# Router products cut into pieces between the query matmuls, with the first norm application and the first scatters moved, in an attention and mixture-of-experts kernel

## What is computed

```python
def attn(x, context, ...):                       # 16 heads of 32
    q = x @ Wq.T + bq; k = context @ Wk.T + bk; v = context @ Wv.T + bv
    scores = einsum('bhtd,bhcd->bhtc', q, k) / sqrt(32)
    return einsum('bhtc,bhcd->bhtd', softmax(scores), v) @ Wo.T + bo

def ffn(x, ...):                                 # 8 experts, the best 2 of each token
    router_weights = softmax(x @ W_router.T + b_router)
    topk_w, topk_idx = top_k(router_weights, 2)
    ...
    expert_out = einsum('bsd,eod->bseo', x, W_experts) + b_experts
    return einsum('bseo,bse->bso', expert_out, router_weights)

x = x + attn(layernorm(x), ctx, ...)
x = x + ffn(layernorm(x), ...)
```

## Time and profile before

| what | value |
| --- | --- |
| timed runs | median 1279.43 us of 3 (1275.38 to 1282.6) |
| profiled execution: span from first to last instruction | 1340.9 us |
| mean granted clock of TensorE | 0.950 |
| busy, PE / DVE / ACT / POOL | 1224.7 / 881.3 / 722.1 / 744.6 us |
| DMA | 239.22 MB, mean 178 GB/s |

### The profile page before, as it was taken

The page is one execution under the profiler, slowest core; times in us unless marked ns, Lnnn a source line. Parts: engine busy times, 40 slices in busy tenths (PEclk is TensorE's granted clock), DMA queues, the critical chain, the costliest instruction groups (busy, mean ns, idle before and its releaser), DMA issues. The chain is left out here.

```text
span 1340.9 us, 36001 instructions
## 1 busy us (share of the span) xinstructions
PE 1224.7 (91%) x11024; PEld 735.1 (55%) x11025; DVE 881.3 (66%) x1933; ACT 722.1 (54%) x1040; POOL 744.6 (56%) x980
## 2 busy tenths in 40 slices
PE   8887999998999989999999986869899999999997
PEld 4445665655655655665655654534354555555454
DVE  4657787877868867867877867545445555555454
ACT  4336875775775775775766662624333333334333
POOL 4003555675675675675675674864644445444545
PEclk9879999999989998989989997889999999999999
DMA  8842664584583574583583573967999989998886
GB/s 267 253 135 65 173 176 153 148 254 142 150 258 130 142 241 152 147 262 131 144 237 115 132 215 109 357 221 156 199 177 184 175 173 188 179 172 155 168 165 133
DMA packets 135547, 239.22 MB, mean 178 GB/s; under 512 B 18440, under 2 KB 49416, under 8 KB 134280
## 3 DMA queue, kind: packets, MB, share of 16 engines
q1 hardware_dynamic: 102391, 161.24, 41.2%
q0 software_dynamic: 29808, 67.73, 25.2%
q10 hardware_dynamic: 3232, 8.68, 1.9%
HBM read 112.00 MB, written 101.40 MB: 159 GB/s over the span
## 5 line engine op out<-in xcount | busy, mean ns | idle before, releaser
L1854 PE MATMUL S<-we_s,wq_s 128*128 x1620 | 376.3, 382 | 12.6 <-DVE att L1832 5.8
L1782 POOL DMA_INDIRECT out<-xn,to x135 | 208.9, 1547 | 212.7 <-DMA out<-xn,to 123.6
L1854 PEld LDWEIGHTS S<-we_s,wq_s 128*128 128x128 f16 x1620 | 158.1, 98 | 180.8 <-issue 22.3
L1172 POOL TENSOR_TENSOR we_s<-P_s,we_s 128x1024 f16<-128x1024 f32 x96 | 204.2, 2136 | 65.6 <-ACT we_s L927 65.3
L1793 ACT ACTIVATE wq_s<-PVp 128x512 f16<-128x512 f32 x137 | 81.6, 597 | 272.4 <-PE PVp L1844 247.1
L1252 POOL DMA_INDIRECT dispatched<-xn,idx x128 | 131.7, 1029 | 92.6 <-ACT xn L620 52.1
L975 DVE TENSOR_REDUCE mx_sb<-S 128x6 f32<-128x924 f32 x160 | 171.3, 1111 | 11.3 <-PE S L726 9.1
L708 PE MATMUL W<-we_s,wq_s 128*128 128x512 f16 x512 | 168.7, 409 | 8.7 <-ACT mT L933 5.3
L746 PE MATMUL W<-wo_s,aT_hi 128*128 128x512 f16 x512 | 164.5, 383 | 2.6 <-DVE aT_lo L953 1.4
L1832 DVE SCALAR_TENSOR_TENSOR att<-S,be_s 128x512 f32<-128x512 f32 x135 | 93.3, 691 | 111.0 <-PE S L1854 101.5
L1810 DVE TENSOR_TENSOR wq_s<-PVp,wq_s 128x512 f16<-128x512 f32 x137 | 94.6, 691 | 38.3 <-ACT wq_s L1793 35.1
(11 more groups left out here) (207 smaller groups left out, 2039.8 us busy)
## 6 DMA issues: line engine op xcount, KB each, us to landing
P_s<-dispatched SPq DMA_DIRECT2D x139, 260.5 KB
we_s<-we_s SPq DMA_DIRECT2D x186, 128.0 KB, 6.0
be_s<-in_x SPq DMA_DIRECT2D x16, 1024.0 KB, 9.1
xR_s<-in_x SPq DMA_DIRECT2D x16, 1024.0 KB
out<-xR_s SPq DMA_DIRECT2D x16, 1024.0 KB
wst<-in_weT SPq DMA_DIRECT2D x16, 512.0 KB, 6.2
we_scratch<-wsp SPq DMA_DIRECT2D x16, 512.0 KB, 5.5
Kst<-k_scratch SPq DMA_DIRECT2D x16, 480.0 KB, 5.1
```

The lines of the kernel that those rows point to most:

```text
L1172: e.tensor_tensor(Pst[1][:, r:r + 2, :], exps(n), Pst[0][:, r:r + 2, :], ALU.subtract).then_inc(pldp, 1)
L1782: e.indirect_dma_start(out, bass.IndirectOffsetOnAxis(ap=to[u][:, :], axis=0), yw[u % YW], None, bounds_check=N - 1, oob_is_err=False, com ...
L1854: m = e.matmul(Yp[:, u % 2, :], gT[u % 2][xp][:, k, :], we_s[:, bass.ds(n * WN + (wp * KC + k) * D, D)], start=(c == 0), stop=(c == 11))
```

## The change

- LA and LB become steps for one token tile each (`pe_LA(e, b, j)`, `pe_LB(e, b, j)`), called by a new `pe_logits`. Pieces 0 and 1 stand behind MT, piece 2 behind Q6 and piece 3 behind Q7. LA leaves its place between ST4 and AT2, and is done for block `bp2`, at the end of the slot before.
- LA moves from bank 1 to bank 0, beside LB (columns 64 to 127). Q9 of the next slot waits for RA, AT2 no longer does; the semaphore for LB is now that of the first reduction (`lbs`).
- DVE: RA runs right after the first reduction of RB, and the rest of RB is a step RL of its own behind it.
- ACT: NY0 and NY1 come before Qh of the first query group, NY2 and NY3 behind it, ahead of NX0; before, all four stood behind the second group and the expert weights' high part.
- POOL: BX3 moves ahead of the first norm's chain NC, so that SC stands right behind the low parts PL7 and PL8.

```diff
@@ -63,7 +63,7 @@
 R32 = 3
 
 BANK = {
-    "ST0": 2, "ST1": 3, "ST2": 2, "Q9": 0, "AT0": 1, "ST3": 3, "AT1": 0, "ST4": 2, "LA": 1, "AT2": 1, "AT3": 0,
+    "ST0": 2, "ST1": 3, "ST2": 2, "Q9": 0, "AT0": 1, "ST3": 3, "AT1": 0, "ST4": 2, "LA": 0, "AT2": 1, "AT3": 0,
     "ST5": 3, "XT0": 0, "O0": 1, "ST6": 2, "R": 0, "ST7": 3, "XT1": 1, "XT2": 0, "ST8": 2, "ST9": 3, "XT3": 1,
     "O3": 0, "Q0": 1, "MX0": 2, "MX1": 3, "Q3": 0, "MX2": 2, "MX3": 3, "O6": 1, "MX4": 2, "MX5": 3, "MX6": 2,
     "MX7": 3, "MX8": 2, "O9": 0, "MX9": 3, "MX10": 2, "MT": 1, "LB": 0, "Q6": 1,
@@ -637,9 +637,9 @@
     HOLDERS = {
         0: (
             ("Q9", 1), ("AT1", -1), ("AT3", -1), ("XT0", 2), ("R", -2), ("XT2", 2), ("O3", -1), ("Q3", 2),
-            ("O9", -1), ("LB", -1),),
+            ("O9", -1), ("LB", -1), ("LA", 2),),
         1: (
-            ("AT0", -1), ("LA", 1), ("AT2", -1), ("O0", -1), ("XT1", 2), ("XT3", 2), ("Q0", 2), ("O6", -1),
+            ("AT0", -1), ("AT2", -1), ("O0", -1), ("XT1", 2), ("XT3", 2), ("Q0", 2), ("O6", -1),
             ("MT", 1), ("Q6", 2),),
         2: (
             ("ST0", 0), ("ST2", 0), ("ST4", 0), ("ST6", 0), ("ST8", 0), ("MX0", 1), ("MX2", 1), ("MX4", 1),
@@ -650,7 +650,7 @@
     }
 
     EMPTIED = {"XT": (t1e, 4), "AT": (ate, 4), "Q": (qle, 4), "O": (x1s, 4), "MT": (mte, 1), "R": (rev, 2),
-               "LA": (lae, 1), "LB": (lbe, 4), "MX": (mxr, 11), "ST": (exd, 10)}
+               "LA": (lae, 1), "LB": (lbs, 1), "MX": (mxr, 11), "ST": (exd, 10)}
 
     def emptied(step, s):
 
@@ -823,36 +823,46 @@
         e.wait_ge(nmd, b.at(4, G + 1))
         pe_T(e, f"AT{G}", b, s, lambda j, k: att[:, j, 4 * k:4 * k + 4, :].rearrange("p h d -> p (h d)"), G, atp)
 
-    def pe_LA(e, b, s):
+    LACOL = NJ * 2 * NE
+
+    def pe_LA(e, b, j):
         bank = BANK["LA"]
-        e.wait_ge(t1e, b.at(4, 4))
-        if b.first:
-            e.wait_ge(p_bk, 5)
-        if free := emptied("LA", s):
-            e.wait_ge(*free)
-        for j in range(NJ):
-            o = W[:, bank, j * 2 * NE:(j + 1) * 2 * NE]
-            for k in range(KC):
-                e.matmul(o.rearrange("p (l e) -> p l e", l=2), xnT[0][:, k, j * P:(j + 1) * P], wr_s[:, :, k, :], start=(k == 0), stop=False)
-            for k in range(KC):
-                m = e.matmul(o[:, 0:NE], xnT[1][:, k, j * P:(j + 1) * P], wr_s[:, 0, k, :], start=False, stop=(k == KC - 1))
-        m.then_inc(lap, 1)
-
-    def pe_LB(e, b, s):
+        if j == 0:
+            e.wait_ge(t1e, b.at(4, 4))
+            if b.first:
+                e.wait_ge(p_bk, 5)
+        o = W[:, bank, LACOL + j * 2 * NE:LACOL + (j + 1) * 2 * NE]
+        for k in range(KC):
+            e.matmul(o.rearrange("p (l e) -> p l e", l=2), xnT[0][:, k, j * P:(j + 1) * P], wr_s[:, :, k, :], start=(k == 0), stop=False)
+        for k in range(KC):
+            m = e.matmul(o[:, 0:NE], xnT[1][:, k, j * P:(j + 1) * P], wr_s[:, 0, k, :], start=False, stop=(k == KC - 1))
+        if j == NJ - 1:
+            m.then_inc(lap, 1)
+
+    def pe_LB(e, b, j):
         bank = BANK["LB"]
-        e.wait_ge(ate, b.at(4, 4))
-        if b.first:
-            e.wait_ge(p_rx, 5)
-        if free := emptied("LB", s):
-            e.wait_ge(*free)
-        for j in range(NJ):
-            o = W[:, bank, j * 2 * NE:(j + 1) * 2 * NE]
-            for k in range(KC):
-                e.matmul(o.rearrange("p (l e) -> p l e", l=2), aT[0][:, k, j * P:(j + 1) * P], wx_s[:, :, k, :], start=(k == 0), stop=False)
-            e.matmul(o[:, 0:NE], ones[:, :], cb_r[:, :], start=False, stop=False)
-            for k in range(KC):
-                m = e.matmul(o[:, 0:NE], aT[1][:, k, j * P:(j + 1) * P], wx_s[:, 0, k, :], start=False, stop=(k == KC - 1))
-        m.then_inc(lbp, 1)
+        if j == 0:
+            e.wait_ge(ate, b.at(4, 4))
+            if b.first:
+                e.wait_ge(p_rx, 5)
+        o = W[:, bank, j * 2 * NE:(j + 1) * 2 * NE]
+        for k in range(KC):
+            e.matmul(o.rearrange("p (l e) -> p l e", l=2), aT[0][:, k, j * P:(j + 1) * P], wx_s[:, :, k, :], start=(k == 0), stop=False)
+        e.matmul(o[:, 0:NE], ones[:, :], cb_r[:, :], start=False, stop=False)
+        for k in range(KC):
+            m = e.matmul(o[:, 0:NE], aT[1][:, k, j * P:(j + 1) * P], wx_s[:, 0, k, :], start=False, stop=(k == KC - 1))
+        if j == NJ - 1:
+            m.then_inc(lbp, 1)
+
+    def pe_logits(e, lb, la, j, s):
+
+        if j == 0:
+            if free := emptied("LB" if lb else "LA", s):
+                e.wait_ge(*free)
+        if la:
+            pe_LA(e, la, j)
+        if lb:
+            pe_LB(e, lb, j)
 
     def act_XTh(e, b, i):
         e.wait_ge(t1p, b.at(4, i + 1))
@@ -996,7 +1006,7 @@
         e.wait_ge(nco[0], b.at(NCO, NCO))
         if b.past(2):
             e.wait_ge(rcq, b.at(1, -1))
-        e.tensor_tensor(lga[p][:, :, :], W[:, BANK["LA"], 0:NJ * 2 * NE].rearrange("p (j e) -> p j e", e=2 * NE),
+        e.tensor_tensor(lga[p][:, :, :], W[:, BANK["LA"], LACOL:LACOL + NJ * 2 * NE].rearrange("p (j e) -> p j e", e=2 * NE),
                         st1[p][:, :].rearrange("p (j o) -> p j o", o=1).broadcast_to([P, NJ, 2 * NE]), ALU.mult).then_inc(lae, 1)
 
     def dve_RB(e, b):
@@ -1004,6 +1014,8 @@
             e.wait_ge(g_set, 9)
         e.wait_ge(lbp, b.at(1, 1))
         e.tensor_reduce(lgs[:, :, :], W[:, BANK["LB"], 0:NJ * 2 * NE].rearrange("p (j l e) -> p j e l", l=2, e=NE), AX, ALU.add).then_inc(lbs, 1)
+
+    def dve_RL(e, b):
         e.wait_ge(lbs, b.at(1, 1))
         e.wait_ge(rqd, b.at(2, 2))
         if b.past(1):
@@ -1374,8 +1386,6 @@
             pe_AT(e, bm1, 1, s)
         if on_b:
             pe_ST(e, b, 4, s)
-        if on_bp1:
-            pe_LA(e, bp1, s)
         if on_bm1:
             pe_AT(e, bm1, 2, s)
             pe_AT(e, bm1, 3, s)
@@ -1461,11 +1471,19 @@
             pe_PV(e, b, 5)
         if on_bp1:
             pe_MT(e, bp1, s)
-        if on_bm1 and not bm1.last:
-            pe_LB(e, bm1, s)
+        lb = bm1 if on_bm1 and not bm1.last else None
+        la = bp2 if on_bp2 else None
+        if lb or la:
+            pe_logits(e, lb, la, 0, s)
+            pe_logits(e, lb, la, 1, s)
         if on_bp2:
             pe_Q(e, bp2, 6, s)
+        if lb or la:
+            pe_logits(e, lb, la, 2, s)
+        if on_bp2:
             pe_Q(e, bp2, 7, s)
+        if lb or la:
+            pe_logits(e, lb, la, 3, s)
 
     def act_slot(e, s):
         bm2, bm1, b, bp1, bp2, bp3 = s + (-2), s + (-1), s, s + 1, s + 2, s + 3
@@ -1517,18 +1535,19 @@
             act_PH(e, b, 9)
         if on_bp3 and not bp3.first:
             act_norm(e, 0, bp3)
+        if on_bm2 and not bm2.last:
+            act_NY(e, bm2, 0)
+            act_NY(e, bm2, 1)
         if on_bp2:
             act_Qh(e, bp2, 0)
+        if on_bm2 and not bm2.last:
+            act_NY(e, bm2, 2)
+            act_NY(e, bm2, 3)
         if on_bp3:
             act_NX(e, bp3, 0)
         if on_bp2:
             act_Qh(e, bp2, 1)
             act_WEh(e, bp2)
-        if on_bm2 and not bm2.last:
-            act_NY(e, bm2, 0)
-            act_NY(e, bm2, 1)
-            act_NY(e, bm2, 2)
-            act_NY(e, bm2, 3)
         if on_bp3:
             act_NX(e, bp3, 1)
         if on_bp1:
@@ -1558,6 +1577,10 @@
             dve_SA(e, bp2, 2)
         if on_bm3 and not bm3.last:
             dve_RB(e, bm3)
+        if on_b:
+            dve_RA(e, b)
+        if on_bm3 and not bm3.last:
+            dve_RL(e, bm3)
         if on_bp2 and bp2.past(2):
             dve_SA(e, bp2, 3)
         if on_b:
@@ -1571,8 +1594,6 @@
             dve_ATl(e, bm2, 0)
             dve_NM(e, bm2, 3)
             dve_ATl(e, bm2, 1)
-        if on_b:
-            dve_RA(e, b)
         if on_bm3 and not bm3.last:
             dve_RM(e, bm3)
         if on_bm2:
@@ -1654,13 +1675,13 @@
             pool_RW(e, bm1)
         if on_bp1:
             pool_PL(e, bp1, 5)
+        if on_b:
+            pool_BX(e, b, 3)
         if on_bp4:
             pool_NC(e, bp4, 0)
         if on_bp1:
             pool_PL(e, bp1, 7)
             pool_PL(e, bp1, 8)
-        if on_b:
-            pool_BX(e, b, 3)
         if on_bm1 and bm1.here(NB - 3):
             pool_SC(e, bm1)
         if on_b and not b.last:
@@ -1991,6 +2012,7 @@
             for u in range(4):
                 dve_tile(e, 0, u)
             dve_RB(e, LAST)
+            dve_RL(e, LAST)
             dve_RM(e, LAST)
             for u in range(4, TU):
                 dve_tile(e, 0, u)
@@ -2028,7 +2050,8 @@
             if ND:
                 e.wait_ge(pldd, ND * NB)
             pe_tile(e, 0, 0)
-            pe_LB(e, LAST, LAST + (-(-1)))
+            for j in range(NJ):
+                pe_logits(e, LAST, None, j, LAST + (-(-1)))
             for u in range(1, TU):
                 pe_tile(e, 0, u)
                 if u == 6:
```

## The result

The changed kernel took 1287.4 us (median of 20 runs, 1281.45 to 1295.83) against 1282.37 for the kernel before (20 runs, 1275.38 to 1289.94): ratio 1.0044, 95% interval 1.0027 to 1.006. So it is slower by 5 us, 10 us above the forecast. That is within the range, by half a microsecond, and within the 0.5% that the prediction called "same" (0.45), but the interval lies wholly above 1, where the forecast had a gain.

A forecast was written before the change was run, and what follows sets the result against it. TensorE was taken to bound each slot at about 44.6 us; with the stall ascribed mostly to recording, only 2 us at the start counted: 1279.4-2 = 1277 us, range 1240 to 1288.

The forecast's parts named there:

- the stall: Idle "issue" time inside LB while the first scatters are issued; at face value 3.8 us a slot, 5.6 with low clock.
- Is that stall in the timed runs?: Step judging that most of the slots' excess belongs to the profile recording, so the forecast gains nothing from the stall's removal.
- 61.2 and 61.5 us: Excess of eleven slots over 44.6 us each, and profiled span over timed median; taken as the same.
- A: Main case, 1277 us, chance 0.50; signs: early scatters, prompt maxima copy, span 1280 to 1310, timed runs within 6 us.
- Pieces cost nothing, LA's 0.95 us is gained at AT1 to AT3: Router pieces in TensorE's slot: 0.95 us gained where LA leaves, 0.95 paid before Q8; net nothing.
- PE's 44.6 us: TensorE taken as the bound of a slot, busy 44.19 of 44.60 us in a slot without scatters.
- -2 us at the start: The longest wait for the read of LA, 3.3 us in the start, goes; 2 us of it counted as gain.
- ACT, POOL: Moved norm steps and BX3 fit into idle time and cost nothing; first scatters begin near 412.3.
- Rival B: The stall is real in timed runs: 1237 or 1218 us, or 1245 to 1258 if half exists; chance 0.28.
- rival D: The stall only moves, scatters now meeting PV4 and PV5: 1270 to 1279 us; chance 0.08.
- Rival C: LA's 0.95 us ahead of Q8 delays the chain to AT1 in 13 slots: 12 us slower, 1291; chance 0.14.

The follow-up runs named there:

- experiment 1: The kernel before, unchanged, timed and profiled again: 1284.14 us, ratio 1.0002, span 1279.5.
- experiment 9: The changed kernel once more, on a chip of the slower kind, against the kernel before: 1314.77 us, ratio 0.9949.
- experiment 4: The changed kernel with TensorE's middle slots as one pass of eight, no jump back, against the kernel before: 1282.13 us, ratio 0.9995.
- 15: The kernel before with TensorE's slot loop in one pass, on a faster chip, against the kernel before: 1279.13 us, ratio 0.9981.
- experiment 11: The kernel before with TensorE's slot loop in one pass, on a slower chip, against the kernel before: 1318.62 us, ratio 0.9972.
- experiment 10: The changed kernel with TensorE's slot loop in one pass, on a slower chip, against the kernel before: 1310.13 us, ratio 0.9907.
- Experiment 17: The changed kernel with its fourth Router piece ahead of Q7 instead of behind it, against the kernel before on a slower chip: 1316.57 us, ratio 0.9879.
- 5: The kernel before with TensorE's middle slots as one pass of eight, on a slower chip, against the kernel before: ratio 0.9979.
- experiments 2: The changed kernel with ScalarE's and GpSimd's order of before, against the kernel before: 1293.84 us, ratio 1.0084.
- 7: The changed kernel with 128 empty semaphore instructions ahead of TensorE's slots, against the kernel before on a slower chip: 1333.0 us, ratio 1.0087.
- 13: The changed kernel with 64 empty semaphore instructions ahead of TensorE's slot loop, one execution on a faster chip: 1292.31 us.
- 14: The changed kernel with 192 empty semaphore instructions ahead of TensorE's slot loop, one execution on a faster chip: 1317.16 us.
- 18: The kernel before with the whole of LB behind Q7, directly ahead of the jump, against the kernel before on a slower chip: 1345.63 us, ratio 1.0086.
- experiments 3: The kernel before with only the new ScalarE and GpSimd order, against the kernel before: 1280.04 us, ratio 0.9989.

## Why the prediction was wrong

*The forecast* was right in kind (no change that half a per cent would tell) and wrong in sign: -2 us, measured +5. Two steps failed: a term left out of the sum, which turned the sign, and the reason for setting the stall aside, which was wrong but left the forecast near the measurement.

*The reason that was wrong* stands in "Is that stall in the timed runs?", where I took it that most of the excess belongs to the recording. The agreement of 61.2 and 61.5 us, on which it leans, was chance. Against experiment 1 the eleven slots hold 44.0 of the 61.4 us by which the two spans differ; another 11.0 us lie behind the first expert transpose (453.4 us to the end, against 442.4), in the stage that recording, as I had it, could hardly have lengthened. PE timelines of before and of experiment 1:

```profile
887.46 1.04 PE L1844 MATMUL PVp<-ident,P_s 128*128 128x128 f32 x8
```

```profile
837.05 1.04 PE L1844 MATMUL PVp<-ident,P_s 128*128 128x128 f32 x8
```

That the stall was missing from the timed runs was true, and 1277 was near only because they ran where it did not occur: that was luck. On the slower kind, with a forecast of -2 us, the change gave -7 (experiment 9). The runs show spans at the times of plain runs with the stall (1324.5 against 1320.46) and without it (1279.5 against 1284.14). So the profile of before and the three timed runs shown must stem from different conditions, and I had not considered that. The signs that I had listed for A all came (scatters, copy, span 1281.3, time within 6 us), and they cannot tell a stall made by recording from one of another chip or hour. The Trainium skill (NOTIFIC — the notification-queue block), § 7.1 Overflow, on which I leant for a recorder that holds its producers back, bears on nothing here. Its § 10 Constraints, capacities, measured rates, by which an implicit record costs no cycles, is what these spans agree with.

*The term that was missing,* and the step that failed for the sign, is the jump. The sum priced the pieces by their 0.94 us and left out where the last of them lands: directly ahead of the loop's jump back. The trace of before had this wait there, which is no row of mine:

```profile
478.80 0.38 PE L708 MATMUL W<-xnT_lo,wq_s 128*128 128x512 f16 x1 [2.21 <-issue]
```

It grew to 5.1 (from 2.4 in experiment 1), and with the half clock behind it the slot lost 6.2 us. By the timed runs the jump's cost went from about 2.4 to about 6.3 us, so 3.9 of the 5 to 5.6 us. What is left is under what these intervals resolve: with no jump in either, the ratios are 0.9995 (experiment 4) and 0.9981 (15), from two sets.

*Pieces cost nothing, LA's 0.95 us is gained at AT1 to AT3* (part 1): right in the rows, AT2's wait gone, AT3's 0.37 us for a forecast 0.4; the last two slots without scatters take 89.0 us together in experiment 1 and 88.9 in the changed kernel. But PE's 44.6 us, from a slot without scatters, was not the bound of a slot with them: GpSimd's low part is late for PV0, by 0.93 us in the slot shown, and the slot is mostly 45.7 to 46.2 with or without the change. So on the faster kind of chip a gain on PE alone in the steady slots could hardly have shown.

*-2 us at the start:* not seen. The 3.3 us wait for the read of LA (at 61.72 us in the profile of before) went, but in its place, at 63.52, stands one of 2.25 us for a low part. The first transpose of the maxima starts at 86.41 and 85.25 us in the two profiles of the kernel before, and at 87.22 and 86.80 in two of the changed kernel.

*ACT, POOL:* right where they were costed at nothing, and perhaps a little better than that (0.9989, not resolved from 1): PE waits 4.6 us in 8 slots for the row of maxima in experiment 1 and 0.5 us in the changed kernel. The scatter's start (7.8 us ahead of the transpose, forecast 8.0) was right.

*Rival B (the stall is real)* is true of the slower kind of chip, in mechanism. Its size was far off: 0.5% in experiment 9, 0.9% without the jump, against 2 to 5%. Without the jump, eleven slots of 48.6 us (experiment 11) became 47.7 (experiment 10) rather than 44.6: as *rival D* had it in kind, the stall in part moved, to AT3's wait for VectorE (19.4 us in 13 waits). *Rival C* had the right sign by the wrong route. On the faster kind of chip AT3 waited 0.37 us, never the microsecond from which C decides; on the slower kind it waited 1.4 to 1.75 us in the slots with scatters but one (experiment 9), and there the changed kernel was the faster one.

## What to carry to other kernels

Before a profile is used against timed runs, compare its span with its own time and with the spread of those runs; if it is 5% off, it is another condition, and both conditions have to be costed. Look for the loop jumps of the bounding engine and for what a change puts right ahead of them: one jump in a 1280 us kernel was most of the loss here. Best of what was run on both kinds of chip: the kernel before with the new ScalarE and GpSimd order and one pass on the faster kind (0.9974; 0.9979 and 0.9967 on the slower), and the changed kernel with its loop in one pass on the slower kind (0.9907; 0.9995 on the faster). Experiment 17 had 0.9879, on a third chip of the slower kind, where neither of these ran.

## What the runs showed of the hardware

Chips, or the hours at which they ran, differ. The same kernel before took 1281.9 to 1283.3 us in the sets on two chips and 1322.0, 1322.9 and 1333.2 on three others, with mean granted clocks of 0.973 to 0.974 in the first two and 0.961, 0.961 and 0.957 in the others. The slots before the first scatters take 44.4 to 44.6 us on both kinds (experiments 1 and 5). The slots with scatters differ, and so does the stretch from the first expert transpose to the end (441.2 us in the changed kernel, 450.2 in experiment 9). In the slots with scatters, news of a burst of small matmuls or of the transpose behind it reaches ACT and DVE late: their readers start 0.75 us (1.94 against 1.19) to 2.25 us (2.96 against 0.71) later than on the faster kind. Whether the matmuls end later than PE's rows say or the news travels late is not told apart, and whether the scatters' traffic itself holds PE up was not tried.

A jump back on TensorE cost 2.1 to 7.2 us of waiting in eleven of the twelve profiled kernels that had it, and 0.48 in the other. From the packet that I take for the fetch to the first matmul are 2.5 to 3.0 us; the rest is how late it starts. The 3.1 us behind each of the eight waits of 5.0 us and more (the changed kernel, experiments 2, 7, 9, 13, 14, 17, 18) ran at clock 0.50, the lower of the two levels (1.2 GHz); behind the 2.1 and 2.4 us of experiments 3 and 1 it stayed at 1.00, and behind the 2.2 us of the profile of before, with its stalls, it was 0.67.
